# Two PSUM accumulations of a gated MLP interleaved matmul by matmul instead of made one after the other

## What is computed

```python
scale = cond @ norm_w.T + 1.0
ms = jnp.mean(x * x, axis=-1, keepdims=True)
h = x * (scale[:, None, :] * jax.lax.rsqrt(ms + EPS))
u = h @ up_w.T                                   # 256 -> 2 x 1024
val, gate = jnp.split(u, 2, axis=-1)
h = val * jax.nn.gelu(gate, approximate=False)   # 1024
hq = act_quant(h)                                # rounded to 8 bits, a step for each token
y = hq @ weight_quant(down_w).T                  # 1024 -> 256, weights -1, 0, 1
return y + x
```

## Time and profile before

| | |
|---|---|
| median of 3 runs | 431.56 us (431.34, 431.56, 1081.13) |
| span of the profiled execution | 429.2 us, granted clock 1.000 |
| busy: PE, PE weight loads, DVE, ACT, POOL | 419.7, 332.7, 283.5, 188.9, 192.7 us |

### The profile page before, as it was taken

One profiled execution on the slowest core, in us unless ns is written; L12 is line 12 of the kernel. 1 busy time (PEld: TensorE's weight loads), 2 busy tenths in 40 slices (PEclk: granted clock), 3 DMA queues, 4 the chain that ended last, 5 costly groups with the idle time before them and its releaser, 6 DMA issues.

```text
span 429.2 us, 7700 instructions
## 1 busy us (share of the span) xinstructions
PE 419.7 (98%) x2062; PEld 332.7 (78%) x2062; DVE 283.5 (66%) x535; ACT 188.9 (44%) x332; POOL 192.7 (45%) x326
## 2 busy tenths in 40 slices
PE   4999999999999999999999999999999999999997
PEld 3777877877777777777777778778778777777885
DVE  4896576575575675675675665765765765756776
ACT  4844444444444444434434444444444444444441
POOL 0665355354354354454453453453553543543520
PEclk9999999999999999999999999999999999999999
DMA  6444435334344234344244343344343343342324
GB/s 217 183 97 124 102 96 122 73 98 122 91 104 118 67 108 122 82 114 96 78 119 122 73 122 75 96 122 109 87 122 74 97 122 94 102 115 71 82 50 124
DMA packets 81816, 45.01 MB, mean 105 GB/s; under 512 B 68304, under 2 KB 68368, under 8 KB 81680
## 3 DMA queue, kind: packets, MB, share of 16 engines
q1 hardware_dynamic: 81808, 44.92, 40.1%
HBM read 20.00 MB, written 8.39 MB: 66 GB/s over the span
## 4 chain that ended last, share of the span: by engine, by line
PE 96%; DMA 1%; SPq 1%; DVE 1%; ACT 0%; issue 0%
PE p_val L611 41%; PE p_gate L611 41%; PE p_y L642 13%; DMA up_raw<-up_w_t 1%; SPq L211 1%; DVE up_lo L434 1%; PE p_gate L642 0%; PE p_val L642 0%; ACT up_hi L360 0%; SPq L213 0%; SPq L178 0%; SPq L214 0%; DVE y_sb L474 0%; SPq L182 0%; PE p_gate L676 0%
## 5 line engine op out<-in xcount | busy, mean ns | idle before, releaser
L519 DVE SCALAR_TENSOR_TENSOR h<-p_val,rstd,gelu 128x512 f32<-128x512 f32 x128 | 95.4, 746 | 126.3 <-PE p_val L611 126.3
L375 ACT ACTIVATE gelu<-p_gate,rstd 128x512 f32<-128x512 f32 x128 | 88.0, 688 | 153.1 <-PE p_gate L611 145.6
L288 POOL TENSOR_TENSOR mean_sq_eps<-mean_sq,rms_eps 128x1 f32<-128x1 f32 x64 | 12.2, 190 | 210.7 <-PE p_val L611 198.6
L353 ACT ACTIVATE q<-q_rounded 128x1024 bf16<-128x1024 f32 x63 | 66.6, 1058 | 71.7 <-DVE q_rounded L557 71.7
L611 PE MATMUL p_gate<-up_hi,a_lo 128*128 128x512 f32 x256 | 86.4, 418 | 2.4 <-ACT up_hi L360 2.4
L611 PE MATMUL p_val<-up_lo,a_hi 128*128 128x512 f32 x256 | 81.0, 397 | 0.3 <-DVE up_lo L434 0.3
L611 PE MATMUL p_val<-up_hi,a_lo 128*128 128x512 f32 x256 | 81.2, 398 | 0.0
L611 PE MATMUL p_gate<-up_lo,a_hi 128*128 128x512 f32 x256 | 81.2, 398 | 0.0
L611 PE MATMUL p_gate<-up_hi,a_hi 128*128 128x512 f32 x256 | 81.1, 398 | 0.0
L611 PE MATMUL p_val<-up_hi,a_hi 128*128 128x512 f32 x256 | 80.8, 397 | 0.0
L543 DVE TENSOR_REDUCE h_max<-h 128x1 f32<-128x1024 f32 x63 | 76.9, 1220 | 2.2
(11 more groups left out here) (55 smaller groups left out, 214.5 us busy)
## 6 DMA issues: line engine op xcount, KB each, us to landing
xt_in<-x_t SPq DMA_DIRECT2D x32, 256.0 KB, 2.8
x_all<-x SPq DMA_DIRECT2D x32, 256.0 KB, 2.9
out<-y_sb SPq DMA_DIRECT2D x32, 256.0 KB, 2.2
up_raw<-up_w_t SPq DMA_DIRECT2D x8, 256.0 KB, 4.7
down_raw<-down_w_t SPq DMA_DIRECT2D x1, 1024.0 KB, 8.0
q_t<-q SPq DMA_TRANSPOSE x63, 3.1
norm_sb<-norm_w_t SPq DMA_DIRECT2D x1, 64.0 KB, 2.2
cond_sb<-cond_t SPq DMA_DIRECT2D x1, 8.0 KB, 2.0
```

The source lines that it names most:

```text
L288: pool.tensor_tensor(mean_sq_eps[:, j:j + 1], mean_sq[:, j:j + 1], rms_eps[:, :], ALU.add).then_inc(pool_step, 1)
L353: act.activation(q[j % 2][:, :], q_rounded[j % 2][:, :], ACT.Copy, bias=-ROUND).then_inc(q_ready, 1)
L375: act.activation(gelu[c][:, :], p_gate[c][:, :], ACT.Gelu, scale=rstd[:, j:j + 1]).then_inc(gelu_done, 1)
L519: nc.vector.scalar_tensor_tensor(h[s][:, c * W:(c + 1) * W], p_val[c][:, :], rstd[:, j:j + 1], gelu[c][:, :], op0=ALU.mult, op1=ALU.mult). ...
```

## The change

In `up()` the two loops change places. Each stationary chunk is used for the gate bank and then at once for the val bank, so the bank that PE writes changes with every matmul. Both waits (for `gelu_done` and `h_done`) now stand ahead of the first matmul of the twelve. The order of the products within a bank changes too: a_lo k0, a_lo k1, then for k0 up_lo and up_hi, then for k1 up_lo and up_hi. The matmuls, their operands and their number stay as they are, and so do the instructions of every other engine.

```diff
-                for which, bank, done, read in ((0, p_gate[c], gate_done, gelu_done), (1, p_val[c], val_done, h_done)):
-                    col = 2 * c + which
-                    if not (first and j == 0):
-
-                        pe.wait_ge(read, NP * (t - 1) + c + 1)
-                    products = [(a_lo[s], up_hi, up_hi_ready), (a_hi[s], up_lo, up_lo_ready), (a_hi[s], up_hi, None)]
-                    for n, (a, w, part) in enumerate(products):
-                        for k in range(KD):
-                            if first and j == 0 and part is not None:
-
-                                pe.wait_ge(part, col * KD + k + 1)
-                            last = nc.tensor.matmul(bank[:, :], a[:, k, :], w[:, col, k, :],
-                                                    start=(n == 0 and k == 0),
-                                                    stop=(n == len(products) - 1 and k == KD - 1))
-                    last.then_inc(done, 1)
+                gate, val = 2 * c, 2 * c + 1
+                if not (first and j == 0):
+
+                    pe.wait_ge(gelu_done, NP * (t - 1) + c + 1)
+                    pe.wait_ge(h_done, NP * (t - 1) + c + 1)
+                products = [(a_lo[s], k, up_hi, up_hi_ready) for k in range(KD)]
+                for k in range(KD):
+                    products += [(a_hi[s], k, up_lo, up_lo_ready), (a_hi[s], k, up_hi, None)]
+                for n, (a, k, w, part) in enumerate(products):
+                    for bank, col, done in ((p_gate[c], gate, gate_done), (p_val[c], val, val_done)):
+                        if first and j == 0 and part is not None:
+
+                            pe.wait_ge(part, col * KD + k + 1)
+                        last = nc.tensor.matmul(bank[:, :], a[:, k, :], w[:, col, k, :],
+                                                start=(n == 0), stop=(n == len(products) - 1))
+                        if n == len(products) - 1:
+                            last.then_inc(done, 1)
```

## The result

The changed kernel takes 434.5 us (median of 4 runs, 433.97 to 435.18) against 431.59 of before: 1.0069 of its time, 95% interval 1.0056 to 1.0082. In a second comparison on one chip it was 434.68 against 431.67, 1.0068 (1.0052 to 1.0084). The ratio leaves out one run of before that took 1081.13 us. The change makes the kernel 0.7% slower: less than the 2% that the prediction calls no change, but clear of the noise. The forecast was 433.2 us, 0.4% slower.

A forecast was written before the change was run, and what follows sets the result against it. The prediction took PE, busy 419.7 of 429.2 us, as the bound. Span 429.2 + 0 (steady) + 1.1 (start) + 0.55 (end) = 430.9 us; with the median 2.3 above span, 433.2 us, range 430.8 to 436.0.

The forecast's parts named there:

- the price of a step: Steady up matmuls on PE: changing bank and repeating a chunk leave each at 0.2333 us, term 0.
- a rival with 0.08: Tile 0: the late first val matmul keeps PE at the lower clock level, +2.4 us, 435.6 us; chance 0.08.
- The first rival: Up matmuls: a repeated chunk is not loaded again or loads cheaper, 14 us less, 419 us, or 411; chance 0.08.
- the second: Up matmuls: changing banks within open sums costs extra; at 0.01 us each 15 us, 448 us; chance 0.06.
- The steady delay of h: Steady tiles: DVE's h starts 0.57 us later, hidden by PE work already queued, cost 0.
- The start: First tiles: no clock cost in tile 0, PE stalls for h of 0.57 and 0.54 us; together +1.1 us.
- I expect the step to 0.233 at about the same time ... Cost 0: Tile 0: PE's clock steps up about when it did before, and the late start is made up; cost 0.
- The two waits for h: Before tiles 2 and 3, PE waits for DVE's late h: 0.57 and 0.54 us.
- The end: Last tile: the last h is 0.57 us later, at most 0.1 us is spare before PE's transposes; +0.55 us.

The follow-up runs named there:

- the edges kernel: Changed kernel with tiles 0 to 3 and 63 in the order of before, tiles 4 to 62 interleaved; 431.5 us against 431.49 of before, ratio 1.0001.
- the repeated chunk: Kernel before, gate then val, but products within each bank in the changed kernel's order, so two of six matmuls repeat a chunk; 431.53 us against 431.52.
- the crossed chunks: Changed kernel, but gate takes one chunk while val takes the other in steady tiles; tiles 0 to 3 and last in old order; 431.4 us against 431.52.
- The filled gap: Changed kernel plus four matmuls into an unused bank between tile 0's first gate and first val matmul; 433.35 us against 431.49 of before, 1.005.
- only the wait moved: Kernel before, same matmul order, but the wait for h_done put ahead of the first gate matmul; 431.8 us against 431.49, ratio 1.0011.

## Why the prediction was right, and where it was not

The direction came out and the price of a step was right. But over a third of the loss (1.27 of 3.4 us) came by a mechanism that the forecast put at nothing and named as a rival with 0.08. That 434.5 lies in the range owes something to luck: the range was wide enough to take in that rival.

**The price of a step: right.** The sum put it at zero from 121 bank changes against 121 steps without one, and named the repeated chunk as what the trace could not show. The 60 tiles from the start of tile 3 on added 0.06 us; the edges kernel, the repeated chunk and the crossed chunks all came out at the time of before. The first rival (cheaper repeated loads, 0.08) and the second (dearer changes in open sums, 0.06) both fall by the table of steps. The Trainium skill (TensorE: Matmul & The Clock Gate, Step-by-step: what each phase is for) says that one can load once and matmul repeatedly. This kernel gains nothing by that, since its program still issues a load with each matmul: PEld counts 2062 loads still. What the Trainium skill tells of cycling through banks (TensorE: Matmul & The Clock Gate, A second HAM failure mode: psum-queue depth-cycling) does not appear here: PE's steady steps stayed at 0.2333 us, the higher level, over all changes of bank.

**The steady delay of h: right in kind.** 0.57 was forecast, 0.64 measured, and it was hidden as said.

**The start: two waits as said, the clock missed, 1.1 forecast and 2.78 measured.** The step that failed first is "I expect the step to 0.233 at about the same time ... Cost 0". The step of the clock came at 14.3, not 11.2, and tile 0 ended 1.27 later. The text had this as a rival with 0.08 and a price of +2.4 (it counted 22 matmuls behind the late one, where 23 are left; with 23 it is +2.8); about half of that price was paid. The filled gap shows that it is this: with the clock up at 9.8 tile 0 ended 1.65 earlier, and the median fell by 1.2. The chance was too low: the argument against it was that 0.6 us of late work (0.9 in the trace) is little beside more than 3. But the trace of before showed one step of the clock, and the step isn't at a fixed distance from the start of unbroken work. It came 3.3 us after it before (7.9 to 11.2), 5.3 with tile 0 in the old order (7.6 to 12.9), 5.7 with only the wait moved (7.9 to 13.6), 5.5 in the changed kernel (8.8 to 14.3), 2.7 with the gap filled (7.1 to 9.8). So how much of the 3.1 us between 11.2 and 14.3 comes of the later start and how much is scatter from one execution to the next, these traces don't tell. What made a late step a loss is that the new order waits for no weights behind its second matmul (in the profiled execution), so nothing is left in which it could hide; the old order with its step at 12.9 or 13.6 hid it behind the last piece of up_lo and POOL's a_lo.

The two waits for h were forecast at 0.57 and 0.54 and measured at 0.65 and 0.86. The first is right. The second missed that DVE's own work is not of fixed length: L454 took 1.55 us (22.96) where it took 1.22 in the old trace, 0.33 more on the very chain that tile 3 waits for. It was as long in the other two fp32r traces with tile 0 interleaved, and 1.22 in bf16; why is open. In addition, behind a wait the second matmul starts 0.30 after the first (23.20 to 23.50) instead of 0.23.

**The end: right.** 0.55 forecast, 0.5 measured; PE idles 0.41 before its transposes, which it did not before.

**The total.** 433.2 forecast, 434.5 measured, inside 430.8 to 436.0. In span the forecast added 1.65 and 3.4 were measured: 1.27 of the missing 1.7 are the clock's, 0.4 are in the two waits for h. In the total only 1.3 are missing, since the forecast put 2.3 us around the span, where the profiled run of the changed kernel (434.41) has 1.8.

## What to carry to other kernels

Before two accumulations are interleaved, look at the steps between banks that the trace already has: if they cost what the others cost, the order of the banks buys nothing in the stream. What the order does change is when each sum is finished and what the first matmul of a group has to wait for. Price that at the unrolled start and end, where the other engines have no slack, and let a sum whose result feeds the longer chain (here gate, then gelu, then h) finish first.

## What was not expected

- The operands' format costs by the column: fp32r 0.2333 us for 512 columns and 0.118 for 256, bf16 0.2158 and 0.109 (the 0.1097 of the earlier trace rows is the chain's mean). The fp32r steps of 512 columns alternate between 0.235 and 0.2315, first and second, whatever chunk or bank they use; the bf16 ones don't. Why is open.
- At the lower level the two cost the same, 0.427 us for 512 columns in the changed kernel in fp32r and in its bf16 form: the surplus is there at the higher level alone.
- The page's granted clock reads full from the first slice, while the steps of 0.427 us up to 14 us show 1.2 GHz. At a kernel's start the distance between matmuls tells the level, the clock row doesn't.
- A few matmuls into an unused bank, while PE waits for weights, brought the higher level 4.5 us earlier (14.3 to 9.8, one trace of each; the scatter without a fill is 2.5 us in the old order, 11.1 to 13.6). It is worth something only where PE is the one that is late: 1.2 us in the changed kernel, nothing in the one before.
